# The last group stored by parity of tokens, and the seventh group's last layer let go by a nearer wait

## The reference, cut to what matters

```python
h = tok_ref(x)                       # 16 signals of 4000 samples -> 249 tokens of 64 features each
h = h + attn_ref(layernorm(h), ...)  # 8 heads, sigmoid instead of softmax
z = layernorm(h)
# feed-forward part, for each token:
all_out = experts(z)     # 4 experts 64 -> 128 -> 64 -> 64, relu between, o = h2 @ eW3 + eb3
shared  = shared_mlp(z)  # 64 -> 64 -> 128 -> 64
gates   = softmax(z @ gW + gb)
topv, topi = top_k(gates, 2); topw = softmax(topv)
out = h + shared + sum(topw * all_out[topi])
```

## Time and profile before

| | us |
|---|---|
| median of 3 runs | 162.69 (162.45 to 162.81) |
| the profiled execution | 162.3 |
| its span, first to last instruction | 160.4 |
| outside of the span | 1.9 |
| PE busy | 147.7 (92%), granted clock 0.989 |
| ACT busy | 117.1 (73%) |
| DVE busy | 110.8 (69%) |
| POOL busy | 55.4 (35%) |

### The profile page before, as it was taken

How to read it: one execution, slowest core, us unless ns; L and a number is a source line. 1 busy time by engine, 2 the same in 40 slices (tenths; PEclk the granted TensorE clock), 3 DMA queues, 4 the chain that set the end, 5 groups by cost and what they waited for, 6 DMA issues and landing times.

```text
span 160.4 us, 6771 instructions
## 1 busy us (share of the span) xinstructions
PE 147.7 (92%) x2888; PEld 85.7 (53%) x2888; DVE 110.8 (69%) x283; ACT 117.1 (73%) x163; POOL 55.4 (35%) x102
## 2 busy tenths in 40 slices
PE   7997866997999999979999999999999999999971
PEld 2486413453566575655666454444656466474661
DVE  2697998989677767647592939762287977768661
ACT  3798874975987998959797898669747757648420
POOL 6000039684997672743517171537000000000000
PEclk9999689999999999999999999999999999999999
DMA  4390000266885875946586302000001011010112
GB/s 122 82 268 0 4 0 0 75 182 148 236 236 166 257 169 183 235 135 190 147 247 193 71 0 37 4 0 4 2 4 36 1 35 34 4 36 5 30 38 64
DMA packets 15634, 14.76 MB, mean 92 GB/s; under 512 B 3692, under 2 KB 14864, under 8 KB 15540
## 3 DMA queue, kind: packets, MB, share of 16 engines
q1 hardware_dynamic: 14836, 13.73, 31.3%
q10 hardware_dynamic: 768, 0.59, 1.2%
HBM read 9.06 MB, written 4.60 MB: 85 GB/s over the span
## 4 chain that ended last, share of the span: by engine, by line
PE 72%; DVE 9%; ACT 9%; DMA 5%; issue 3%; POOL 0%; DVEq 0%; POOLq 0%
PE ps L483 15%; PE ps L501 14%; PE ps L612 9%; PE ps L628 8%; PE ps L512 5%; PE ps L687 4%; DMA YS<-y_stage 4%; PE ps L638 3%; ACT probs L1309 2%; PE ps L678 2%; PE ps L709 2%; PE ps L353 2%; ACT area L1244 2%; PE ps L615 2%; DMA y_stage<-YP 1%
## 5 line engine op out<-in xcount | busy, mean ns | idle before, releaser
L1309 ACT ACTIVATE probs<-ps 125x1000 f32<-125x1000 f32 x64 | 61.4, 1007 | 11.4 <-PE ps L483 8.3
L501 PE MATMUL ps<-probs,xn 124*32 124x250 f32 (+1 forms) x512 | 39.8, 375 | 0.3 <-ACT probs L1309 0.2
L483 PE MATMUL ps<-YS,XT 128*32 128x500 f16 x448 | 35.0, 376 | 1.1 <-DMA YS<-y_stage 0.9
L501 PEld LDWEIGHTS ps<-probs,xn 124*32 124x32 f32 (+1 forms) x512 | 16.4, 109 | 12.5 <-issue 2.3
L1330 ACT ACTIVATE area<-ps,wf 128x500 f32<-128x500 f32 x32 | 20.5, 672 | 2.3 <-PE ps L612 2.3
L1344 ACT ACTIVATE area<-ps,wf 128x500 f32<-128x500 f32 x20 | 13.5, 677 | 9.7 <-PE ps L628 7.0
L931 DVE COPY ZS<-ps 128x250 f32<-128x250 f32 x32 | 12.9, 412 | 9.3 <-PE ps L501 9.1
L483 PEld LDWEIGHTS ps<-YS,XT 128*32 128x32 f16 x448 | 11.0, 96 | 11.3 <-ACT probs L1309 4.2
L628 PE MATMUL ps<-area,wf 128*64 128x500 f32 x64 | 16.1, 584 | 0.0
L912 DVE CAST YP<-ps 128x500 f16<-128x500 f32 x14 | 9.5, 677 | 8.9 <-PE ps L442 8.9
L612 PE MATMUL ps<-X2T,w1h 128*64 128x500 f16 x64 | 12.4, 385 | 0.0
(11 more groups left out here) (170 smaller groups left out, 262.1 us busy)
## 6 DMA issues: line engine op xcount, KB each, us to landing
YS<-y_stage SPq DMA_DIRECT2D x28, 250.0 KB, 3.6
y_stage<-YP SPq DMA_DIRECT2D x10, 250.0 KB, 3.1
tower_out<-res SPq DMA_DIRECT2D x7, 124.0 KB
wf<-wf_in SPq DMA_DIRECT2D x1, 648.0 KB, 5.8
y_stage<-YP SPq DMA_DIRECT2D x5, 125.0 KB, 4.0
wa<-wa_in SPq DMA_DIRECT2D x1, 512.0 KB, 5.1
y_stage<-YP ACTq DMA_DIRECT2D x3, 125.0 KB, 2.9
ch<-ch_in SPq DMA_DIRECT2D x1, 160.0 KB, 4.9
```

Of the source, the lines that this page charges most:

```text
L483: last = mm(ps[k0:k1, 2 * (n % 2) + j, 0:TG].rearrange("p (h n) -> p h n", h=2), XT[:, g % 3, (2 * bb + cj) * P + k0:(2 * bb + cj) * P + k ...
L501: last = mm(ps[R * hh:R * hh + R, 4 + bb, half * TB:(half + 1) * TB], xn[0:keys, 4 * g + 2 * bb + cj, :], probs[0:keys, n % 3, hh, :], sta ...
L1309: fn(probs[:, n % 3].rearrange("p (j h) n -> p j (h n)", j=2), ps[0:P, 2 * (n % 2):2 * (n % 2) + 2, 0:TG], ACT.Sigmoid, scale=SCORE_SCALE) ...
```

## The change

Group 7's last layer runs over t in the order 0, 2, 1, 3 and its banks are chosen by parity, so the first half that is done is parity 0 of both signals, and `finish_last(c)` adds and stores parity c. Each parity goes in two transfers with runs of 256 bytes, 112 partitions from SP and the rest from ACT, partition 124 with parity 0; the transfer L339 is gone. PE's wait before `layer3(6)` becomes `scaled >= 22`, the count that the second multiplication of `finish_experts(5)` sets. `finish_sums(5)` stands behind both `weigh(7, ...)` on DVE. The store of group 6 moves from SP's queue to ACT's.

```diff
--- before.py
+++ after.py
@@ -243,6 +243,19 @@
 
             return 7 if g == 1 or (g, k) == (2, 1) else 6
 
+        def store(eng, g):
+
+            eng.wait_ge(res_done, g + 1)
+            eng.dma_start(out[2 * g:2 * g + 2, 0:NW - 1, :].rearrange("b (p c) f -> p b (c f)", c=2),
+                          res[0:P - 1, g % 2].rearrange("p b c f -> p b (c f)")).then_inc(out_done[g % 2], 16)
+            eng.dma_start(out[2 * g:2 * g + 2, NW - 1, :].rearrange("(a b) f -> a b f", a=1),
+                          res[P - 1:P, g % 2, :, 0, :]).then_inc(out_done[g % 2], 16)
+
+        def last_tokens(c, p0, p1):
+
+            first_token = out[NB - 2, c]
+            return bass.AP(first_token.tensor, first_token.offset + 2 * p0 * F, [[2 * F, p1 - p0], [NW * F, 2], [1, F]])
+
         def x2_ready(eng, g):
 
             if g in BY_PE:
@@ -326,21 +339,14 @@
             read_back(NG - 1, 1)
             x2_turn(4)
             x2_turn(5)
-            for g in range(NG - 1):
-                sp.wait_ge(res_done, g + 1)
-                sp.dma_start(out[2 * g:2 * g + 2, 0:NW - 1, :].rearrange("b (p c) f -> p b (c f)", c=2),
-                             res[0:P - 1, g % 2].rearrange("p b c f -> p b (c f)")).then_inc(out_done[g % 2], 16)
-                sp.dma_start(out[2 * g:2 * g + 2, NW - 1, :].rearrange("(a b) f -> a b f", a=1),
-                             res[P - 1:P, g % 2, :, 0, :]).then_inc(out_done[g % 2], 16)
-            for b in range(2):
-                sp.wait_ge(res_done, NG + b)
-                sp.dma_start(out[NB - 2 + b, 0:2 * EVEN, :].rearrange("(p c) f -> p (c f)", c=2),
-                             res[0:EVEN, 2, b].rearrange("p c f -> p (c f)")).then_inc(last_out, 16)
-            sp.dma_start(out[NB - 2:NB, NW - 1, :].rearrange("(a b) f -> a b f", a=1),
-                         res[P - 1:P, 2, :, 0, :]).then_inc(last_out, 16)
+            for g in range(NG - 2):
+                store(sp, g)
+            for c in range(2):
+                sp.wait_ge(res_done, NG + c)
+                sp.dma_start(last_tokens(c, 0, EVEN), res[0:EVEN, 2, :, c, :]).then_inc(last_out, 16)
             sp.wait_ge(out_done[0], 32 * (NG // 2))
             sp.wait_ge(out_done[1], 32 * (NG // 2 - 1))
-            sp.wait_ge(last_out, 5 * 16)
+            sp.wait_ge(last_out, 4 * 16)
 
 
         @block.tensor
@@ -697,10 +703,10 @@
                 pe.wait_ge(mix_done, 2 * (g - LATE) + 2)
                 pe.wait_ge(l2_act, 3 * g + 3)
                 if g == LATE:
-                    pe.wait_ge(res_done, g)
-                for t in range(4):
+                    pe.wait_ge(scaled, 4 * (LATE - 1) + 2)
+                for t in (0, 2, 1, 3) if g == NG - 1 else range(4):
                     b, c = divmod(t, 2)
-                    bank = LAST_BANK[b] if g == NG - 1 else OUT_BANK
+                    bank = LAST_BANK[c] if g == NG - 1 else OUT_BANK
                     for q0, q1 in ((0, F), (F, P)):
                         mm(ps[q0:q1, bank, t * F:(t + 1) * F], WT[:, 2 * g + b, q0:q1], b3s[:, c * F:(c + 1) * F],
                            start=True, stop=False)
@@ -710,7 +716,7 @@
                                       H2[:, g % 2, k, t * P + q0:t * P + q1],
                                       wf[:, WF["w3"][0] + k * F:WF["w3"][0] + (k + 1) * F],
                                       start=False, stop=(k == 2))
-                    if t == 3 or (g == NG - 1 and t == 1):
+                    if t == 3 or (g == NG - 1 and t == 2):
                         last.then_inc(l3_mm, 1)
 
 
@@ -1136,11 +1142,12 @@
                 dve.wait_ge(l3_mm, 2 * (g - 1))
                 v.tensor_tensor(H2[:, g % 2, k, :], H2r[:, g % 2, k, :], ps[:, spread_bank(g, k), 0:TG], ALU.mult).then_inc(mix_done, 1)
 
-            def finish_last(b):
-                dve.wait_ge(l3_mm, NG + LATE + b)
-                rows = slice(2 * NB - 4 + 2 * b, 2 * NB - 2 + 2 * b)
-                v.tensor_tensor(res[:, 2, b], ps[0:P, LAST_BANK[b], 2 * b * F:2 * (b + 1) * F].rearrange("p (t f) -> p t f", f=F),
-                                h2[:, rows, :], ALU.add).then_inc(res_done, 1)
+            def finish_last(c):
+                dve.wait_ge(l3_mm, NG + LATE + c)
+                v.tensor_tensor(res[:, 2, :, c, :],
+                                ps[0:P, LAST_BANK[c], 0:4 * F].rearrange("p (b c f) -> p b c f", b=2, c=2)[:, :, c, :],
+                                h2[:, 2 * NB - 4:2 * NB, :].rearrange("p (b c) f -> p b c f", c=2)[:, :, c, :],
+                                ALU.add).then_inc(res_done, 1)
 
             sst = Steps(dve, scaled)
 
@@ -1202,7 +1209,7 @@
                     routing_take(1)
                 if g == LATE:
                     weigh(g, 0)
-                if 2 <= g < LATE + 2:
+                if 2 <= g <= LATE:
                     finish_sums(g - 2)
                 if g == NG - 1:
                     weigh(g, 0)
@@ -1216,6 +1223,8 @@
                     gate_gap(1)
                 if LATE <= g < NG:
                     weigh(g, 1)
+                if g == NG - 1:
+                    finish_sums(g - 2)
                 if 1 <= g <= LATE:
                     finish_base(g - 1)
                 if g == 4:
@@ -1357,10 +1366,10 @@
                         gap_sigmoids(1)
                 if g + 1 < NG:
                     relu1(g + 1, 3)
-            for b in range(2):
-                act.wait_ge(res_done, NG + b)
-                act.dma_start(out[NB - 2 + b, 2 * EVEN:NW - 1, :].rearrange("(p c) f -> p (c f)", c=2),
-                              res[EVEN:P - 1, 2, b].rearrange("p c f -> p (c f)")).then_inc(last_out, 16)
+            store(act, NG - 2)
+            for c in range(2):
+                act.wait_ge(res_done, NG + c)
+                act.dma_start(last_tokens(c, EVEN, P - c), res[EVEN:P - c, 2, :, c, :]).then_inc(last_out, 16)
 
 
         @block.gpsimd
```

## The result

The change makes the kernel slower: median 163.39 us (22 runs) against 162.53 for the kernel before (22 runs of the same occasion), ratio 1.0068 with a 95% interval of 1.0039 to 1.0097. On a second occasion it was 1.0079 (1.0035 to 1.0123). Forecast were 163.2 and slower. The level fits better than the change: forecast was +0.5 us, measured is 0.86 between the medians and 1.1 by the ratio. Runs in a slower state (one of each kernel took 188 and 190 us) are left out of the ratio.

The account below looks back on a forecast made before the run. The last packet was taken to set the end: four engines busy 0.40 + 2.85 + 0.50 + 0.1 = 3.85 us from 155.86, 0.59 later than before, making 163.28, taken down to 163.2 us; range 163.0 to 163.6, 8 in 10 162.2 to 163.7.

Parts of the forecast that it names:

- PE's stall is a wait for the sums; it goes: PE's 0.81 us idle before layer3(6) was put on res_done >= 6, not ACT's L1344; gain 0.79 us.
- DVE: Group 5's sums move to 153.42 to 155.03, from 151.90 to 153.51; additions by parity cost at most 0.1 us each.
- Issues: SP issues group 5's store 1.52 us later, ACT group 6's at 155.40; the last issue ends 1.2 us earlier.
- Two stores on the same four engines: Stores of groups 5 and 6 share four engines, which work 3.85 us from 155.86; last packet +0.59 us; chance 0.55.
- The rule of the Trainium skill: A transfer uses the lowest-numbered engines, the largest number up to 16 dividing its slowest dimension: 4 for 124, 16 for 112.
- the rows of the two stores: Transfers of groups 5 and 6 on four engines: 0.40 us at the slow start, then 2.85 us at 82 GB/s.
- the slow start: First 0.40 us of the stores' packets, 20 KB; group 6's early packets were expected to fill part of it.
- What was left behind the stores: On the four engines: parity rows of 256 bytes 0.50 us, ACT's pieces, small stores and completions about 0.1 us.
- The fixed tail: From the last packet to the end of the span: 1.28 us, taken as unchanged.
- Rival A: ACT's store gets four other engines, so the two stores don't meet; last packet -0.9 us, 161.8 us; chance 0.18.
- Rival B: Two queues draw more from each engine, 26.7 GB/s; last packet -0.27 us, 162.4 us; chance 0.25 with what lies between.
- Rival C: PE's gain is absent, layer3(6) stays at 153.66 and parities come 0.79 us later; same 163.2 us; no chance given.

Follow-up runs that it names:

- e4: Kernel before with only PE's wait ahead of layer3(6) changed, to scaled >= 22; ratio to the kernel before 0.9923.
- e1: Changed kernel with finish_sums(5) put back ahead of weigh(7, 0) on DVE; ratio to the kernel before 0.9916, on another occasion 0.9953.
- e8: Kernel before with PE's nearer wait and finish_sums(5) behind both weigh(7, ...), stores as before; ratio to the kernel before 1.0051.
- e2: Changed kernel with the stores of groups 5 and 6 each cut into 112 and 12 partitions; ratio to the kernel before 1.0015.
- e3: Changed kernel with group 6's store issued by SP, behind group 5's, in place of ACT; ratio to the kernel before 0.9995.
- e6: e1 with all of group 6's store on SP; ratio to the kernel before 0.9967.
- e7: Changed kernel with group 5's store alone cut into 112 and 12 partitions; ratio to the kernel before 0.9965.
- e10: e2 with eight more waits on SP, all long satisfied, ahead of the stores; ratio to the kernel before 0.9949.
- e11: e7 with eight more waits on SP, all long satisfied, ahead of the stores; ratio to the kernel before 0.9983.
- e5: e1 with group 6's store cut: 112 partitions from ACT, 12 and the small one from SP; ratio to the kernel before 0.9978.

## Why the prediction was right, point by point

- *PE's stall is a wait for the sums; it goes.* Right: +0.87 at L711, 0.85 at the last addition, forecast 0.79; e4 shows it with one line changed. That the chain blamed ACT was the coincidence I took it for: L711 no longer stalls, though ACT's L1353 is where it was.
- *DVE.* Right: sums end at +2.84 by forecast, +2.82 in the trace. Additions by parity took 0.29, as before.
- *Issues.* Group 5's store forecast at +2.86, measured +2.84; group 6's +3.20 and +3.18. Parity 0 was 0.38 later than forecast (+4.18 for +3.80), SP's gap; it decided nothing here, since the four engines had group 6's rows until +7.38.
- *Two stores on the same four engines.* Right, and shown three ways: ACT's first packet came 2.44 us after its issue in place of 0.91; taking the lateness away (e1) took away all of the loss, and putting it alone into e4 (e8) brought it; spreading the stores (e2) moved both in 1.6 us in place of 3.75.
- *The rule of the Trainium skill on which engines a transfer uses* (page "DMA: Bandwidth & Descriptors", section "Why a DMA increments its semaphore by 16 and not by 1") carried over to ACT's queue, as the trace now shows: when ACT's rows are nearly alone (159.25 to 159.60) they keep 0.29 of 16 engines busy, and before that they had waited for SP's.
- *The size.* Forecast +7.51 for the last packet, measured +7.86: 0.35 more. The term that was too small is the rows of the two stores, 3.25 us in the sum and about 3.75 measured (+3.63 to +7.38): group 5's took 2.28 in place of 1.7. e3, with about 1.7, says that ACT's issues beside it have to do with that. Nor did early packets of group 6 fill the slow start, for which the forecast was taken from 163.28 to 163.2: none moved before +5.62. What was left behind the stores, 0.60 in the sum, took 0.48; some of the short rows had gone before. By share and pace a row of 256 bytes keeps an engine busy for some 18 ns (0.24 of 16 at 55 GB/s) and one of 512 for some 28 (0.29 at 84), about two thirds of it.
- *The fixed tail.* Wrong, and it hid part of the miss. The sum put 1.28 behind the last packet; it was 1.12, and 0.84 to 1.53 in the experiments. From mark to end the forecast was +8.79 and the trace has +8.98, only 0.19 more, because one error took back part of the other: luck. Nor was the last packet of the kernel before one of the big rows: those were over by +6.70, and the end was L339's. Against them the four engines are 1.16 us later.
- *Rival A* fell (ACT's store does not get other engines). *Rival B* fell: where both queues have work left for the four alone (159.25 to 159.60), 55 of 64 packets are ACT's and the pace is 84 GB/s, as with one store; while ACT's store was issued and SP's rows moved (157.40 to 158.06), there were only 60. *Rival C*, the late sums with the old wait, was not run.
- *What I had not seen*: the PE gain of the wait needs the multiplication moved as well; with the sums ahead 0.3 of it is lost (e4).

In time, the trace has 0.93 us at the last packet and 0.77 from mark to end, beside 0.0068 x 162.5 = 1.1 us (0.6 to 1.6) in the runs. The forecast change of 0.5 lies below that interval: the way and the level, 163.2 for 163.39, were right, the size was taken too small, and the level owes something to a kernel before that measured 162.53 here in place of 162.69.

## What to carry to other kernels

How many DMA engines a store uses sets much of its price: here 124 partitions went over four engines in 1.7 us while twelve stood idle, and two such stores close together took 3.4 us from one queue (e3) and 3.75 from two. Before moving a store or what feeds it, look at the transfers' share of 16 engines in its stretch, and ask what the engines it uses are doing at its new time. And when a wait is made shorter, keep whatever hides a slow transfer where it is: here one line (e4) gave 0.8%, and a second, well-meant move behind it turned that into a loss of 0.5% (e8).

## What the runs showed of the hardware that I had not expected

- Issues from ACT are dearer than from SP: the same 124-partition store 0.52 to 0.53 us against 0.26, the small one 0.71 against 0.57 to 0.59 (changed kernel, and e1 and e6, where little else is issued).
- SP stood still for 0.44 to 0.47 us behind issues of group 5's store wherever it could not hide it (changed kernel, e2, e3, e7, e8), and eight idle waits ahead took the gap to 0.04 and 0.05 (e10, e11). The issue of 12 partitions took SP 0.32 us on its own (e5) and 0.42 to 1.27 right behind one of 112.
- In the changed kernel and its repeat the rows of the second queue did not take turns with the first from the start: group 6's began at +5.62 and +5.47, when group 5's, which ended at +5.91 and +5.94, were nearly through. Whether the engines served them so or the rows came to them late is not shown.
- The time from the last packet to the end of the program varied between kernels from 0.84 to 1.53 us.
